# Graph network kernel: the adjacency transposed on VectorE from a second, block-ordered load, with new orders on every engine

## Reference, cut to what matters

```python
h = relu(norm(x)); x = x + attention(h, adj)      # 4 heads, mask adj > 0.5
h = relu(norm(x)); x = x + relations(h, adj)      # max over 7 products: adj @ , adj.T @ , shifts, identity
h = relu(norm(x)); x = x + convolution(h, adj)    # relu(D^-1/2 (adj + I) D^-1/2 (h W^T + b))
h = relu(norm(x)); x = x + laplacian(h, adj)      # softplus(norm(h) W_self + (I - S_out adj S_in) norm(h) W_neigh)
```

## Time and profile before

| | |
|---|---|
| runs | 696.86 us median of 3 (696.1 to 698.95) |
| profiled execution | 696.5 us, of which the span from first to last instruction 694.6 us |
| busy over the span | PE 646.9 us, PEld 522.8, DVE 535.5, ACT 544.5, POOL 376.3 |
| mean granted TensorE clock | 0.973 of full speed |
| moved by DMA | 44.47 MB |

### The profile page before, as it was taken

How to read it: one execution, slowest core, us unless ns; L and a number is a source line. 1 busy time by engine, 2 the same in 40 slices (tenths; PEclk the granted TensorE clock), 3 DMA queues, 4 the chain that set the end, 5 groups by cost and what they waited for, 6 DMA issues and landing times. The chain is left out here.

```text
span 694.6 us, 20320 instructions
## 1 busy us (share of the span) xinstructions
PE 646.9 (93%) x7476; PEld 522.8 (75%) x7476; DVE 535.5 (77%) x1641; ACT 544.5 (78%) x1271; POOL 376.3 (54%) x435
## 2 busy tenths in 40 slices
PE   5469899999999999999999999999999999998865
PEld 3455778879697878879697878789697767877654
DVE  5776768897979798897979797897977769796541
ACT  6677678888889898888889798888888785875243
POOL 2655565574746565574846565664833563536321
PEclk9697999999999999999999999999999999999996
DMA  7222040222222022222222111222222102100001
GB/s 215 91 67 73 3 138 3 77 78 78 77 78 76 11 77 72 76 78 79 78 77 78 51 48 59 77 78 78 77 63 77 64 17 62 66 14 1 15 1 31
DMA packets 39532, 44.47 MB, mean 64 GB/s; under 512 B 4545, under 2 KB 23050, under 8 KB 39434
## 3 DMA queue, kind: packets, MB, share of 16 engines
q1 hardware_dynamic: 38802, 42.95, 19.6%
q10 hardware_dynamic: 632, 0.22, 0.1%
HBM read 38.83 MB, written 4.33 MB: 62 GB/s over the span
## 5 line engine op out<-in xcount | busy, mean ns | idle before, releaser
L498 POOL TENSOR_TENSOR rstd<-ve,half_neg 128x4 f32<-128x4 f32 (+1 forms) x67 | 89.4, 1334 | 211.6 <-DVE ve L1434 65.4
L820 ACT ACTIVATE side<-d_all,sd 128x512 bf16<-128x512 f32 x256 | 163.8, 713 | 38.4 <-DVE pos L1330 30.9
L1856 PEld LDWEIGHTS ps<-part,pos 128*128 128x128 bf16 x3072 | 100.9, 97 | 9.9 <-issue 6.3
L1856 PE MATMUL ps<-part,pos 128*128 128x66 bf16 x3072 | 103.1, 193 | 0.6 <-DVE pos L1330 0.6
L1330 DVE TENSOR_TENSOR pos<-side,none 128x2048 bf16<-128x2048 bf16 x64 | 80.6, 1259 | 8.6 <-ACT side L820 7.7
L1392 DVE TENSOR_REDUCE best<-ps 128x128 f32<-128x896 f32 x64 | 69.4, 1088 | 18.8 <-PE ps L1952 17.4
L2054 PE MATMUL ps<-u,adj_tr 128*128 128x128 f32 x512 | 62.2, 281 | 1.9 <-ACT u L920 1.9
L2054 PEld LDWEIGHTS ps<-u,adj_tr 128*128 128x128 f32 x512 | 60.4, 197 | 3.1 <-ACT u L920 3.1
L1842 PEld LDWEIGHTS ps<-part,nmask 128*128 128x128 bf16 x1536 | 52.8, 99 | 12.3 <-issue 12.1
L1900 PE MATMUL ps<-adj_tr,h 128*128 128x512 f32 x128 | 60.5, 617 | 0.6 <-ACT h L729 0.6
L1914 PE MATMUL ps<-adj_in,h 128*128 128x512 f32 x128 | 57.7, 592 | 0.0
(11 more groups left out here) (166 smaller groups left out, 1522.3 us busy)
## 6 DMA issues: line engine op xcount, KB each, us to landing
adj_in<-in_adj SPq DMA_DIRECT2D x16, 1024.0 KB, 5.9
d_all<-d_dram SPq DMA_DIRECT2D x64, 256.0 KB, 3.8
x_in<-in_x SPq DMA_DIRECT2D x16, 256.0 KB, 3.4
out_y<-y_out SPq DMA_DIRECT2D x15, 256.0 KB, 2.5
d_dram<-sd_t SPq DMA_DIRECT2D x64, 2.0 KB, 1.4
w_sb<-in_L_gnn_W SPq DMA_DIRECT2D x7, 64.0 KB, 2.4
b_sb<-in_L_gnn_b SPq DMA_DIRECT2D x1, 256.0 KB, 3.3
out_y<-y_out SPq DMA_DIRECT2D x2, 128.0 KB, 1.8
```

Of the source, the lines that this page charges most:

```text
L498: G.tensor_tensor(rstd[:, cut], ve[:, cut], half_neg[:, cut], ALU.pow).then_inc(power, 1)
L820: last = A.activation(side[:, t, :], d_all[:, h, :], ACT.Sign, bias=sd[:, 0, h, t:t + 1])
L1856: last = mm(ps[:, B_HEADS[q] + i // 2, o:o + VAL], pos[h % 2][:, t, i * P:(i + 1) * P], parts[n][:, t, h, :], start=False, stop=(i % 2 == ...
```

## The change

The transposes leave TensorE and the copies with sums leave ScalarE. SP loads the adjacency a second time, into one new buffer adj_blk, in four transfers a graph: each brings a set of 32 columns of every 128 to 32 partitions, in runs of 32 floats (128 bytes). Four DVE transposes of 128x512 (each works on 32x32 blocks) then give adj_tr. ScalarE makes the column sums by a pass over adj_tr. SP's scores_in is split into head 0 and the rest. Banks are assigned anew, the waits on PSUM banks follow them, some small buffers share memory differently, and the orders of all five engines are new. The functions norm3 and its centering are unchanged.

```diff
-DEPTH = 9
-B_ADJ = (5, 2, 5, 2)
-B_HEADS = (4, 0)
-B_SUMS, B_H1T, B_AH, B_ATH = 1, 0, 3, 2
-B_REL = (2, 0, 2, 4)
+DEPTH = 10
+B_HEADS = (0, 2)
+B_SUMS, B_H1T, B_AH, B_ATH = 0, 3, 5, 0
+B_REL = (0, 2, 4, 2)
...
+            @of_graph
+            def load_blocks(g):
+                if g.has(1):
+                    sync.wait_ge(adj_sb, g.before(1).all(1))
+                for b in range(T):
+                    sync.dma_start(adj_blk[b * (P // T):(b + 1) * (P // T), :, :].rearrange("r t (m c) -> r (t m) c", c=P // T),
+                                   adj[g.n, :, :].rearrange("(m r) (t b c) -> r t m b c", r=P // T, b=T, c=P // T)[:, :, :, b, :]
+                                   ).then_inc(s_blk, 16)
...
             load_features(at(0))
-            load_adjacency(at(0))
-            first_data()
             load_features(at(1))
-            load_weights()
-            load_adjacency(at(1))
-            load_laplace()
+            load_blocks(at(0))
             scores_out(at(0))
             load_features(at(2))
-            scores_in(at(0))
+            scores_in((0,))(at(0))
+            scores_in((1, 2, 3))(at(0))
+            load_adjacency(at(0))
+            load_blocks(at(1))
+            load_adjacency(at(1))
...
+            for s in range(7, GRAPHS + DEPTH - 1 - 7):
+                scores_out(at(s - 5))
+                load_features(at(s - 2))
+                scores_in((0,))(at(s - 5))
+                scores_in((1, 2, 3))(at(s - 5))
+                store(at(s - 9))
+                load_blocks(at(s - 4))
+                load_adjacency(at(s - 4))
...
-                    A.activation(adj_tr[g.three][:, t, :], bank(B_ADJ[t]), ACT.Copy,
-                                 accum_out=sums[g.three][:, 0, t:t + 1]).then_inc(adj_sb, 1)
+            @of_graph
+            def column_sums(g):
+                act.wait_ge(adj_sb, g.all(1))
+                act.wait_ge(row_sum, g.all(1))
...
+                for t in range(T):
+                    last = A.activation(junk[:, t, :], adj_tr[g.three][:, t, :], ACT.Copy,
+                                        accum_out=sums[g.three][:, 0, t:t + 1])
+                last.then_inc(col_sum, 1)
...
+            @of_graph
+            def adjacency(g):
+                dve.wait_ge(s_blk, g.all(16 * T))
...
+                for t in range(T):
+                    last = V.transpose(adj_tr[g.three][:, t, :], adj_blk[:, t, :])
+                last.then_inc(adj_sb, 1)
...
+            degrees(at(0))
             top_score(at(1))
+            adjacency(at(1))
+            bias_rows()
+            edge_parts()
             weights(at(1))
...
+                norm1(at(s - 5))
+                adjacency(at(s - 4))
                 top_score(at(s - 4))
+                laplace(at(s - 7))
+                no_edges(at(s - 4))
                 weights(at(s - 4))
...
+                largest(2)(at(s - 5))
+                largest(3)(at(s - 5))
+                residual1(at(s - 5))
+                head(2)(at(s - 4))
+                norm2(at(s - 5))
+                pair(0)(at(s - 4))
+                head(3)(at(s - 4))
+                scores(at(s - 3))
+                softplus(at(s - 7))
+                pair(1)(at(s - 4))
+                attention(at(s - 4))
+                residual0(at(s - 4))
...
-            def adjacency(t):
-                @of_graph
-                def piece(g):
-                    pe.wait_ge(s_adj[g.two], g.loaded())
...
-                    for i in range(T):
-                        last = tr(bank(B_ADJ[t])[:, i * P:(i + 1) * P], adj_in[g.two][:, i, t * P:(t + 1) * P], ident[:])
-                    last.then_inc(adj_ps, 1)
...
+                conv_bias(at(s - 5))
+                conv_linear(at(s - 5))
+                laplace_product(at(s - 6))
+                top_rows(at(s - 3))
+                conv_product(at(s - 5))
+                top_all(at(s - 3))
+                h1_transposed(at(s - 4))
+                product_ath(at(s - 4))
+                product_ah(at(s - 4))
+                project(at(s - 2))
+                relation(0)(at(s - 4))
+                relation(1)(at(s - 4))
+                mean_value(at(s - 2))
+                relation(2)(at(s - 4))
+                no_edges(0)(at(s - 3))
+                relation(3)(at(s - 4))
+                z_transposed(at(s - 5))
+                head(0)(at(s - 3))
+                no_edges(1)(at(s - 3))
+                head(1)(at(s - 3))
+                laplace_linear(at(s - 5))
+                head(2)(at(s - 3))
+                row_sums(at(s - 3))
+                head(3)(at(s - 3))
+                h2_transposed(at(s - 4))
+                h0_transposed(at(s - 1))
```

More of the change, by code:

```diff
@@ L1550, in _ @@
             scores(at(2))
-            node_scales(at(1))
-            residual0(at(1))
-            top_score(at(2))
-            norm1(at(1))
-            weights(at(2))
-            degrees(at(2))
-            norm0(at(5))
-            no_edges(at(2))
-            part_rest(at(2))
-            edges_negative(at(2))
-            residual2(at(0))
-            part_lo(at(2))
-            head(0)(at(2))
-            norm3(at(0))
+            residual0(at(1))
+            norm1(at(1))
+            adjacency(at(2))
@@ new lines, in _ @@
+            part_lo(at(2))
+            largest(2)(at(1))
+            largest(3)(at(1))
+            residual1(at(1))
+            norm2(at(1))
+            head(2)(at(2))
+            norm0(at(5))
+            degrees(at(2))
+            head(3)(at(2))
+            pair(0)(at(2))
+            pair(1)(at(2))
+            scores(at(3))
+            attention(at(2))
+            residual0(at(2))
+            for s in range(7, GRAPHS + DEPTH - 1 - 7):
+                norm1(at(s - 5))
+                adjacency(at(s - 4))
@@ L1600, in _ @@
-            largest(2)(at(11))
-            largest(3)(at(11))
-            head(3)(at(12))
-            residual1(at(11))
-            norm2(at(11))
-            pair(1)(at(12))
-            scores(at(13))
-            attention(at(12))
-            laplace(at(10))
-            residual0(at(12))
-            top_score(at(13))
-            norm1(at(12))
-            weights(at(13))
-            softplus(at(10))
-            node_scales(at(12))
-            part_rest(at(13))
-            degrees(at(13))
@@ L2222, in _ @@
-            head(3)(at(14))
+            no_edges(0)(at(2))
+            mean_value(at(3))
+            head(0)(at(2))
+            z_transposed(at(0))
+            no_edges(1)(at(2))
+            head(1)(at(2))
+            laplace_linear(at(0))
+            head(2)(at(2))
+            head(3)(at(2))
+            h2_transposed(at(1))
+            conv_bias(at(1))
+            conv_linear(at(1))
+            row_sums(at(2))
+            laplace_product(at(0))
+            h0_transposed(at(4))
+            top_rows(at(3))
@@ new lines, in _ @@
+            conv_product(at(1))
+            h1_transposed(at(2))
+            top_all(at(3))
+            product_ath(at(2))
+            product_ah(at(2))
+            project(at(4))
+            relation(0)(at(2))
+            relation(1)(at(2))
+            relation(2)(at(2))
+            no_edges(0)(at(3))
+            relation(3)(at(2))
+            mean_value(at(4))
+            head(0)(at(3))
+            z_transposed(at(1))
+            head(1)(at(3))
+            no_edges(1)(at(3))
+            laplace_linear(at(1))
```

992 lines of the change are left out of this document (376 added, 616 removed).

## The result

| | before | after |
|---|---|---|
| median of the runs | 696.47 us (12 runs, 695.05 to 699.81) | 692.62 us (12 runs, 690.97 to 694.94) |
| ratio | | 0.9938, interval 0.9923 to 0.9952 |
| span of the profiled execution | 694.6 us | 690.7 us |

What follows compares the result with a forecast made beforehand. The prediction took the middle to be bound by TensorE's work alone. From 696.5 us, -25.8 for the transposes, +3.0 for DVE's surviving waits and +4.0 for the start gave 677.7, say 678 us, range 662 to 697.

Steps and rivals of the forecast that it cites:

- Every microsecond taken off it is gained until the next engine is met: In the middle, bound by TensorE's work alone, work taken off TensorE shortens the period, 38.89 to 37.05 us.
- The price of the transposes: On TensorE, four pieces of 0.46 us cost 1.84 us a graph; removing them for 14 graphs gives -25.8 us.
- The waits of DVE: Most of DVE's waits for head and relation results should go; 0.25 us booked for 12 periods, +3.0 us.
- DVE's demand: DVE's need per period in the middle rises from 33.6 to 36.1 us, against a pace of 37.05.
- ScalarE hidden: ScalarE's sum passes over SBUF replace its PSUM copies at +0.07 us a graph, hidden, with 3.3 us left.
- The 39 us given for two passes: DVE's demand per period if each DVE transpose passed the data twice, 1.2 us each.
- The load: The second adjacency load: 27 ns a run, 13.8 us a graph plus about 2; costs nothing under 55 ns.
- The 112 us: Estimated load time a graph if the skill page's 19 times for strided DMA transposes applied; the prediction argued it differs here.
- The start: Relation(0) of graph 0 comes later because c_rows arrive at 68 us: +4 us, between -3 and +8.
- The end: In the tail, graph 15's chain stays and TensorE's 21 us of idle is kept, +-4.
- (a): Rival: DVE shares the pace, 1 to 1.6 us of waits left, period 37.8 to 38.5, 684 to 693 us; 18%.
- (b): Rival: slower by DVE, whose waits survive whole; period 41.4 us, time 730 us; 10%.

## Why the prediction was wrong

- **"Every microsecond taken off it is gained until the next engine is met"** is the first step that failed. The price of the transposes was right (1.83 us from start to start in the kernel before). But they were also cover for answers of other engines: the old kernel with a quarter of them gave 0.79 us for 1.28, with nothing added to DVE. A stretch in which TensorE is busy all the time isn't thereby bound by its work alone.
- **The waits of DVE.** "An engine that is late finds its inputs ready, so most of them should go" is the step that cost most. The forecast pace of 37.3 leaves room for 0.5 us a period of waits for TensorE beside the 0.7 for GpSimd's xf (36.1 + 0.7 + 0.5). Measured were 18.7 us in 8.15 periods, 2.3 each, beside 6.1 us for xf, 0.7 each: 36.2 + 0.7 + 2.3 make 39.2, the measured period. A late engine finds its inputs ready only if the engine that makes them doesn't depend on it. Here TensorE is itself late, since it waits for part_lo (1.62 us), and DVE's lateness comes back to it half a period later. So it isn't one engine or the other that sets the pace, but DVE's 19.9 us and TensorE's 19.3 one behind the other.
- **DVE's demand** (36.1 forecast; 35.3 busy and about 0.9 of small gaps measured), **the transposes** (0.63; 0.61) and **ScalarE hidden** (33.85 of 39.25) were right. One thing in DVE's demand I hadn't asked: which of its instructions would stand beside GpSimd's in the new order. Two did, for 0.9 us each; in the old order two instructions of degrees had (about 1.0 and 0.92 us, 0.3 now), so the total is nearly right while the delay now sits in the loop. The 39 us given for two passes is 38.4 by the prediction's own terms (33.6 + 4.8); nothing hangs on it.
- **The load** was right: hidden, and at 18.8 ns a run below the 27 taken; only its issue on SP was sized too small. The Trainium skill, in "VectorE: DVE Perf Modes", section "The three transpose paths", compares a plain DMA with strides to the DMA's own transpose, and no run here makes that transpose. The 112 us that were estimated from its 19 times don't show: the runs cost about 9.6 us of all 16 engines a graph (8192 x 18.8 ns / 16), and the plain load in their place changed nothing.
- **The start** was sized +4 and measured +1 to graph 2. The forecast took norm1 of graph 0 at its old time, 48.8; in the new order it was done at 43.3, so c_rows came 6 us sooner than I had it. That half the clock follows the wait for it wasn't in the sum.
- **The end** I took as kept. The last three periods and the tail gave 9.2 us, more than the whole gain; three times 1.84, 5.5 us, of it was in the sum. For the rest, TensorE's new list has less work of other graphs between graph 15's pieces; this is what I suppose, no run took it apart, and the cause stays open.
- **Rivals.** (a), DVE sharing the pace, had the time (684 to 693), but by luck: its period was 37.8 to 38.5 with 1 to 1.6 us of surviving waits, and 39.25 and 2.3 were measured. Start and end, which came out better than the sum had them, made up for it. Its mechanism was near, though it saw DVE's total as the limit and not a loop. (b), slower with all waits surviving, gave 41.4 and 730: nearly what the moved work does in the old orders (41.7 and 741). The prediction had two effects as alternatives where one comes on top of the other: the moved work costs 2.8 us a period, and the new orders give 2.5 back.

In sum: forecast -25.8 and +3.0 for the middle and end, +4.0 for the start. Measured: +1.0 to graph 2, +4.2 in ten periods, -6.9 in the last three, -2.3 in the tail, together -4.0 (the spans differ by 3.9). For the ten periods the forecast was -16 (ten times -1.84 + 0.25): there it failed, by 20 us. In all 15 are missing, since start and end came out better than forecast.

## What to carry to other kernels

In a software pipeline over several engines the period can be set by a loop that passes from engine to engine and back, and then neither busy total shows it; look for two engines that each wait for the other at a fixed place, and add up the two stretches between the waits. Work moved to an engine with idle time is paid in full if it lands inside such a loop, and a move of a few tiny instructions out of it can be worth more than a microsecond of work taken off the busiest engine. After each such move expect the next loop a few tenths behind, and look at what stands ahead of its links in every list.

## What the runs showed of the hardware

- VectorE instructions were held up while GpSimd worked on tensors: residual2, with two SBUF inputs, took 1.57 us beside values where it took 0.68 in the kernel before, and a 128x4 subtraction, also with two, 826 ns on the average where it took 226 in another place. One input doesn't always spare an instruction: a 128x16 one took 0.95 us beside a GpSimd addition where it took 0.17, while BATCH_NORM_STATS took its usual 0.87 us.
- VectorE transposes 128x512 float32 in 32x32 blocks in 0.61 us from start to start; an addition of that size takes 0.66 us on the average in the kernel before.
- DMA reads in runs of 128 bytes took an estimated 18.8 ns of an engine each, so 1 MB in such runs takes about 9.6 us of all 16 (8192 x 18.8 / 16).
- A wait of 5.35 us on TensorE was followed by four microseconds at a granted clock of 0.50 and four at 0.71. With a wait of 0.98 us in its place the clock stayed at 1.00 and the kernel was 2.7 us shorter, though the relation started no sooner. With the transposes issued twice, three microseconds at 0.51 followed a wait of 2.58 us.
